# Turning two of three gathered tiles on VectorE instead of TensorE in a mixture-of-experts stage

## The reference, cut to what matters

```
x  = x + tanh(g_xattn) * align(ctx, layernorm(x))
xf = layernorm(x);  logits = xf @ gate_w.T
w, sel = top_k(logits, 2);  w = softmax(w)
out[n] = sum over the 2 chosen e of w[n,e] * (expert_w[e] @ xf[n])
x  = x + tanh(g_ffn) * out
```

## Time and profile before

| | us |
|---|---|
| median of 3 runs (599.56, 602.33, 602.07) | 602.07 |
| the profiled execution, its own time | 599.65 |
| its span | 597.9 |
| TensorE busy | 457.6 (77%) |
| VectorE busy | 307.6 (51%) |
| ScalarE busy | 263.0 (44%) |
| GpSimd busy | 225.5 (38%) |

### The profile page before, as it was taken

The page is one execution under the profiler, slowest core; times in us unless marked ns, Lnnn a source line. Parts: engine busy times, 40 slices in busy tenths (PEclk is TensorE's granted clock), DMA queues, the critical chain, the costliest instruction groups (busy, mean ns, idle before and its releaser), DMA issues. The chain is left out here.

```text
span 597.9 us, 8208 instructions
## 1 busy us (share of the span) xinstructions
PE 457.6 (77%) x2029; PEld 271.4 (45%) x2029; DVE 307.6 (51%) x1635; ACT 263.0 (44%) x508; POOL 225.5 (38%) x214
## 2 busy tenths in 40 slices
PE   8989655477232304687996989999999999999980
PEld 7989543254122201343443544444454444445440
DVE  7778799999998885898678411101111010111000
ACT  6538778854735402892653223322233332223320
POOL 5550222000000000003428565766657665767522
PEclk9999868668565655796997999999999999999995
DMA  8965334640046001777999686878868787878743
GB/s 289 353 189 190 86 85 117 187 98 2 0 160 263 1 1 36 288 245 231 296 260 309 116 164 122 149 134 144 138 114 153 130 142 136 139 122 152 118 53 35
DMA packets 61386, 88.88 MB, mean 149 GB/s; under 512 B 24933, under 2 KB 25189, under 8 KB 61181
## 3 DMA queue, kind: packets, MB, share of 16 engines
q0 software_dynamic: 16048, 37.31, 35.8%
q1 hardware_dynamic: 38701, 42.64, 21.8%
q10 hardware_dynamic: 6592, 8.42, 4.5%
HBM read 48.92 MB, written 39.43 MB: 148 GB/s over the span
## 5 line engine op out<-in xcount | busy, mean ns | idle before, releaser
L1973 PE MATMUL psum<-big,work 128*128 x560 | 257.1, 602 | 4.3 <-ACT work L1627 4.3
L697 POOL DMA_INDIRECT stage<-x_rows,row_ids x71 | 70.0, 986 | 224.1 <-DVE row_ids L1173 176.0
L1973 PEld LDWEIGHTS psum<-big,work 128*128 128x128 f32 x560 | 102.9, 194 | 108.0 <-issue 108.0
L1323 DVE TENSOR_TENSOR part_scale<-stage,st 128x1 f32<-128x1 f32 x62 | 10.0, 162 | 201.2 <-DMA stage<-x_rows,row_ids 201.2
L717 POOL DMA_INDIRECT out_dram<-prow,row_ids x34 | 61.3, 1802 | 36.0 <-ACT prow L1638 14.2
L717 POOL DMA_INDIRECT out_dram<-tokens,row_ids x36 | 57.2, 1589 | 41.3 <-DMA out_dram<-tokens 15.5
L1638 ACT ACTIVATE tokens<-psum,tile_shares 128x512 f32<-128x512 f32 x36 | 24.7, 687 | 98.4 <-issue 70.5
L1638 ACT ACTIVATE prow<-psum,tile_shares 128x512 f32<-128x512 f32 x34 | 23.3, 687 | 86.8 <-issue 78.6
L1947 PEld LDWEIGHTS psum<-ident,stage 128*128 128x128 f32 x284 | 35.6, 143 | 40.6 <-issue 33.7
L1756 PE MATMUL psum<-ident,stage 128*128 128x128 f32 x128 | 27.7, 401 | 33.3 <-ACT big L1526 20.5
L1627 ACT COPY work<-psum 128x512 f32<-128x512 f32 x71 | 41.0, 578 | 19.2 <-PE psum L1947 14.8
(11 more groups left out here) (388 smaller groups left out, 649.7 us busy)
## 6 DMA issues: line engine op xcount, KB each, us to landing
tokens<-in_x_dram SPq DMA_DIRECT2D x16, 1024.0 KB, 11.8
stage<-in_L_ffn_expert_w_dram ACTq DMA_DIRECT2D x8, 1024.0 KB, 5.6
out_dram<-tokens SPq DMA_DIRECT2D x8, 1024.0 KB, 9.1
x_rows<-tokens SPq DMA_DIRECT2D x7, 1024.0 KB, 7.3
tokens<-dist_rows SPq DMA_DIRECT2D x52, 64.0 KB, 2.1
dist_rows<-work SPq DMA_DIRECT2D x16, 160.0 KB, 2.0
dist_rows<-prow SPq DMA_DIRECT2D x5, 256.0 KB, 10.5
stage<-x_rows,row_ids POOLq DMA_INDIRECT x71
```

Of the source, the lines that this page charges most:

```text
L697: pool.indirect_dma_start(out=xin[:, n % UX, :], out_offset=None, in_=x1_d[0:T, :] if n < FA else x1_d[:, :], in_offset=bass.IndirectOffse ...
L1973: ins = nc.tensor.matmul(psum[:, UP + n % UP, :], xinT[:, n % UX, c, :], expT[:, bass.ds(own, 1), c, :].rearrange("p o d -> p (o d)"), sta ...
```

## The change

Of the second list, tiles 12 and 13, 15 and 16, and so on to 69 and 70 (20 pairs, `PAIRED` holds the first of each) aren't turned by TensorE. VectorE turns a pair with 16 transposes: a block of 32 partitions of the gathered tiles, in blocks of 32x32 numbers, goes to 32 partitions of `pairT`, so that the four chunks of 128 columns of both tiles are done in one instruction (32 partitions x 256 numbers). `pairT` is three pairs in `x[:, 4:10, :]`, and the expert matmuls read it directly. Tiles 0 to 11 and 14, 17, ..., 68 (31, `TURNED`) go as before. The second list gathers into six buffers (UZ = 6) in an order in which the two of a pair lie side by side, with semaphores of their own, six tiles ahead instead of four.

```diff
+    UZ = 6
+    UD = 6
+    HOMES = (4, 5, 3, 1, 2, 0)
+    PAIRED = [n for n in range(FA + 3, NSEQ - 1) if (n - FA) % 3 == 0]
+    TURNED = [n for n in range(NSEQ) if n not in PAIRED and n - 1 not in PAIRED]
...
-        xin = stagef[:, 0:UX * RW].rearrange("p (h c) -> p h c", c=RW)
+        xin = stagef[:, 0:UZ * RW].rearrange("p (h c) -> p h c", c=RW)
+        pairT = x[:, GT:GT + UD, :]
...
+        def home(n):
+            return n % UX if n < FA else HOMES[(n - FA) % UZ]
+
+        def landed(n):
+            return (s_xi[n % UX], 16 * (n // UX + 1)) if n < FA else (s_zi[(n - FA) % UZ], 16 * ((n - FA) // UZ + 1))
+
+        def pair_of(n):
+            return PAIRED.index(n if n in PAIRED else n - 1)
+
+        def tileT(n, c):
+            if n in TURNED:
+                return xinT[:, n % UX, c, :]
+            return pairT[:, (2 * pair_of(n) + (n not in PAIRED)) % UD, c * P:(c + 1) * P]
...
-                if n >= UX:
+                if UX <= n < FA:
                     pool.wait_ge(s_yt, n - UX + 1)
-                if n - UX >= FA:
-                    pool.wait_ge(s_scale, n - UX - FA + 2)
+                if FA <= n < FA + UZ and home(n) < UX:
+                    pool.wait_ge(s_yt, max(m for m in range(FA) if home(m) == home(n)) + 1)
+                if n - UZ >= FA:
+                    if n - UZ in TURNED:
+                        pool.wait_ge(s_yt, TURNED.index(n - UZ) + 1)
+                    else:
+                        pool.wait_ge(s_dt, pair_of(n - UZ) + 1)
+                    pool.wait_ge(s_scale, n - UZ - FA + 2)
...
+            AHEAD = [n + UX for n in range(FA - UX + 1)] + [FA + 2, FA + 3, FA + 5]
+            AHEAD += [min(n + UZ, NSEQ) for n in range(FA, NSEQ + 1)]
...
-                if n + UX < NSEQ:
-                    gather(n + UX)
+                for m in range(*AHEAD[n:n + 2]):
+                    gather(m)
...
+            def turn_pair(n):
+
+                d = 2 * pair_of(n)
+                v.wait_ge(*landed(n))
+                v.wait_ge(*landed(n + 1))
+                if d >= UD:
+                    v.wait_ge(s_y, PAIRED[(d - UD) // 2] + 2)
+                for a in range(P // NB):
+                    for g in range(P // NB):
+                        got = xin[NB * g:NB * (g + 1), home(n):home(n) + 2, 0:C].rearrange("p t (q a i) -> p t q a i", q=CH, i=NB)
+                        to = pairT[NB * a:NB * (a + 1), d % UD:d % UD + 2, :].rearrange("p t (q n) -> p t q n", q=CH)
+                        ins = v.transpose(to[:, :, :, NB * g:NB * (g + 1)], got[:, :, :, a, :])
+                ins.then_inc(s_dt, 1)
...
             for n in range(FA, NSEQ):
+                if n in PAIRED:
+                    turn_pair(n)
                 tile_share(n)
...
             def copy_in(n):
+                if n not in TURNED:
+                    return
+                i = TURNED.index(n)
...
             def turn(n):
-                pe.wait_ge(s_xi[n % UX], 16 * (n // UX + 1))
-                if n >= UP:
-                    pe.wait_ge(s_yc, n - UP + 1)
+                if n not in TURNED:
+                    return
+                i = TURNED.index(n)
+                pe.wait_ge(*landed(n))
+                if i >= UP:
+                    pe.wait_ge(s_yc, i - UP + 1)
...
+            def tile_ready(n):
+                if n in TURNED:
+                    pe.wait_ge(s_yc, TURNED.index(n) + 1)
+                else:
+                    pe.wait_ge(s_dt, pair_of(n) + 1)
```

More of the change, by code:

```diff
@@ L397, in flamingo_block @@
         s_xi = [sem(f"tile_gathered{h}") for h in range(UX)]
+        s_zi = [sem(f"second_tile_gathered{h}") for h in range(UZ)]
+        s_dt = sem("pair_turned")
         s_yt = sem("tile_transposed")
@@ L692, in gather @@
                         pool.wait_ge(s_sto[b], 16)
-                if n >= UX:
+                if UX <= n < FA:
                     pool.wait_ge(s_yt, n - UX + 1)
-                if n - UX >= FA:
-                    pool.wait_ge(s_scale, n - UX - FA + 2)
+                if FA <= n < FA + UZ and home(n) < UX:
[6 more added lines that the diff above has]
+                    pool.wait_ge(s_scale, n - UZ - FA + 2)
                 pool.indirect_dma_start(
-                    out=xin[:, n % UX, :], out_offset=None, in_=x1_d[0:T, :] if n < FA else x1_d[:, :],
+                    out=xin[:, home(n), :], out_offset=None, in_=x1_d[0:T, :] if n < FA else x1_d[:, :],
                     in_offset=bass.IndirectOffsetOnAxis(ap=rows_ids[:, n:n + 1], axis=0),
-                ).then_inc(s_xi[n % UX], 16)
+                ).then_inc(landed(n)[0], 16)
             def add(n):
@@ L1316, in ids @@
                                                  [psum[:, 7, 0:1].ap[0], [2 * JB, K], [1, JB]])))
+            def turn_pair(n):
[10 more added lines that the diff above has]
+                ins.then_inc(s_dt, 1)
             def tile_share(n):
                 j = n - FA
-                v.wait_ge(s_xi[n % UX], 16 * (n // UX + 1))
+                v.wait_ge(*landed(n))
                 v.wait_ge(s_scale, n - FA + 1)
-                lnk(v.tensor_tensor(part_scale[:, :], xin[:, n % UX, C + 1:C + 2], kinds[:, 1, j:j + 1], ALU.mult))
-                v.scalar_tensor_tensor(scale[:, n:n + 1], xin[:, n % UX, C:C + 1], kinds[:, 0, j:j + 1], part_scale[:, :],
+                lnk(v.tensor_tensor(part_scale[:, :], xin[:, home(n), C + 1:C + 2], kinds[:, 1, j:j + 1], ALU.mult))
+                v.scalar_tensor_tensor(scale[:, n:n + 1], xin[:, home(n), C:C + 1], kinds[:, 0, j:j + 1], part_scale[:, :],
                                        ALU.mult, ALU.add).then_inc(s_scale, 1)
@@ L1623, in copy_in @@
             def copy_in(n):
+                if n not in TURNED:
+                    return
+                i = TURNED.index(n)
                 if n >= UX:
                     act.wait_ge(s_y, n - UX + 1)
-                act.wait_ge(s_yt, n + 1)
-                nc.scalar.copy(xinT[:, n % UX, :, :].rearrange("p c n -> p (c n)"), psum[:, n % UP, :]).then_inc(s_yc, 1)
+                act.wait_ge(s_yt, i + 1)
+                nc.scalar.copy(xinT[:, n % UX, :, :].rearrange("p c n -> p (c n)"), psum[:, i % UP, :]).then_inc(s_yc, 1)
             def copy_out(n):
@@ L1942, in turn @@
             def turn(n):
-                pe.wait_ge(s_xi[n % UX], 16 * (n // UX + 1))
-                if n >= UP:
-                    pe.wait_ge(s_yc, n - UP + 1)
+                if n not in TURNED:
[4 more added lines that the diff above has]
+                    pe.wait_ge(s_yc, i - UP + 1)
                 for c in range(CH):
-                    ins = nc.tensor.transpose(psum[:, n % UP, c * P:(c + 1) * P], xin[:, n % UX, c * P:(c + 1) * P],
+                    ins = nc.tensor.transpose(psum[:, i % UP, c * P:(c + 1) * P], xin[:, home(n), c * P:(c + 1) * P],
                                               ident[:, :])
                 ins.then_inc(s_yt, 1)
+            def tile_ready(n):
[3 more added lines that the diff above has]
+                    pe.wait_ge(s_dt, pair_of(n) + 1)
             def owned(n):
@@ L1956, in last_expert @@
             def last_expert(n, own):
-                pe.wait_ge(s_yc, n + 1)
+                tile_ready(n)
                 pe.wait_ge(s_ye, n - UP + 1)
@@ L1960, in last_expert @@
                     for c in range(CH):
-                        ins = nc.tensor.matmul(psum[:, UP + n % UP if h == 0 else 4, h * HC:(h + 1) * HC], xinT[:, n % UX, c, :],
+                        ins = nc.tensor.matmul(psum[:, UP + n % UP if h == 0 else 4, h * HC:(h + 1) * HC], tileT(n, c),
                                                expT[:, bass.ds(own, 1), c, h * HC:(h + 1) * HC].rearrange("p o d -> p (o d)"),
@@ L1972, in expert @@
                 for c in range(CH):
-                    ins = nc.tensor.matmul(psum[:, UP + n % UP, :], xinT[:, n % UX, c, :],
+                    ins = nc.tensor.matmul(psum[:, UP + n % UP, :], tileT(n, c),
                                            expT[:, bass.ds(own, 1), c, :].rearrange("p o d -> p (o d)"),
```

## The result

The changed kernel takes 582.12 us (median of 4 runs, 581.6 to 583.19), the kernel before 600.98 us in the same comparison: ratio 0.9689, 95% interval 0.9657 to 0.972. The forecast was 583.5 us. The profiled execution has a span of 579.8 us, 18.1 less than before.

What follows compares the result with a forecast made beforehand. TensorE was taken to bound the second list's stage. 18.2 us from turns removed, less 0.7, is 17.5 us: 582.2 from the profiled execution, 584.6 from the median, so 583.5 us forecast, range 580 to 596 us.

Steps and rivals of the forecast that it cites:

- The price of a turn: TensorE, second list: each turn costs 0.43 us by tile distance; 36 tiles after the first two give 15.5 us.
- The first pair: Tiles 12 and 13: without turns and the wait for gather 12, tile 12 can start 2.74 us earlier.
- 0.7 us for a late landing: First pair: half of the 1.5 us wait that the late bound for gather 13's landing would give, taken off.
- The sum: Whole kernel: 18.2 us gained up to tile 67, less 0.7, is 17.5 us.
- The cover I gave (74%): VectorE in steady state: 8.0 us of work per three tiles, 74% of TensorE's 10.75 us.
- cover of 8.8 us: GpSimd, add 9 to add 67: alone it could reach add 67 at 543.3, TensorE releases it at 552.1.
- 7 x 2.70: GpSimd: seven flagged adds each wait 2.70 us more for the add ahead to land.
- The end: Last adds: a chain of flagged adds waiting for landings; what TensorE gains after tile 67 is worth nothing.
- A: GpSimd becomes the bound through slower landings and longer flagged-add waits: smaller gain, 589 or 597 us; chance 0.17.
- B: VectorE becomes the bound: 0.69 us a transpose, 12.3 us per three tiles, about 612 us; chance 0.10.
- C: VectorE's transposes hold GpSimd: 0.13 us an instruction, 589 us, or some 80 us lost if held throughout; chance 0.07.
- D: No change: possible only by a long stall at the first pair with the clock halved, 5 to 8 us; chance 0.04.

Runs made afterwards that it cites:

- dead turns: Changed kernel, with four unread TensorE transposes of the identity for each paired tile in place of the turns removed: 599.56 us, ratio 0.9984.
- seven of nine: Changed kernel with 7 of 9 tiles turned by VectorE, still six gather buffers and gathers six tiles ahead: 583.27 us, ratio 0.9706.
- two kernels with 24 transposes: Changed kernel with eight extra unread transposes a pair: each right before its twin, 592.43 us; all eight behind the sixteen, 611.89 us.
- with sums: Changed kernel with four unread VectorE sums of two SBUF inputs among each pair's last transposes: 584.27 us, ratio 0.9737.
- four of five: Changed kernel with four of five tiles turned by VectorE, five gather buffers in turn, gathers five tiles ahead: 588.36 us, ratio 0.9804.

## Why the prediction was right

*The price of a turn.* The mechanism forecast is the one seen: TensorE is full, and what it no longer has to do comes off the time (dead turns bring it back). From tile 12's matmuls to tile 68's it was 216.86 us before (352.63 in the earlier trace rows, 569.49 in the earlier trace rows) and is 200.61 now (350.93 to 551.54). 37 turns are gone in between: 16.25 us, 0.44 each, for 0.43 in the prediction. Taking it from the distance of tiles, and not from the 273 ns of each transpose, is what made the sum.

*The first pair.* Timeline of GpSimd where the second list begins, before and after:

```profile
331.24 1.01 POOL L697 DMA_INDIRECT stage<-x_rows,row_ids  x1 [2.34 <-DVE half_row_ids L1313]
```

```profile
332.43 1.02 POOL L725 DMA_INDIRECT stage<-x_rows,row_ids  x1 [2.32 <-DVE half_row_ids L1343]
```

Counted from this first gather, tile 12 starts 2.9 us earlier, for 2.74 predicted. I had taken off 0.7 us for a late landing; it was not needed, but with 0.6 us to spare it was near.

*The sum.* From the first gather to add 67 it was 239.02 us before (331.24 to 570.26) and is 220.32 now (332.43 to 552.75): 18.7 us, for 18.2 in the sum before the 0.7 was taken off. The medians differ by 18.9. So the step that was off is the 0.7, and the 1.4 us between forecast and result is less than single executions of the kernel before differ by (599.56 to 602.33 us). The base had some luck in it: the forecast lay midway between two times of the kernel before, 599.65 and 602.07, and the median of the comparison, 600.98, lies there too.

*VectorE.* 436 ns for a transpose and 0.449 from one to the next, 7.2 us a pair, for 0.42 and 6.7. The length was right to 4% by the row of the same size; the step from one to the next is 13 ns more, which was left out. 31.97 of 40 us for "about 30". The cover I gave (74%) is 80%: (7.18 + 1.4) of 10.75 us.

*GpSimd.* Same durations, and it did wait for ScalarE before add 67. But the cover of 8.8 us was a term that I had too large. Seven waits for a landing cost 22.4 us beyond the gaps of 0.30, not 7 x 2.70 = 18.9: six of the flagged adds come 5.9 to 6.4 us after the one ahead, and the seventh (544.59) waits 4.88 us, since no gather stands between it and the add ahead any more. Another 1.7 us went to the shares that queue behind the first pair's turn (the gather at 351.55), where I had put nothing. What is left at the end is the wait for ScalarE, 2.0 us beyond the gap. That was enough here, and it is gone with seven of nine.

*The end.* Turns of tiles 69 and 70 give nothing: add 67 to 68 is 5.65 us in the changed kernel, longer than any tile.

*The rivals.* A did not decide in this kernel, and does in the next step up. B did not decide either, since 0.449 us an operation is under the 0.59 from which I had the gain shrink. The two kernels with 24 transposes bear out its limits: 11.19 us per three tiles, as much as 16 operations of 0.61 us would make, shrank the gain (592 us), and 12.15, or 0.67 us an operation, gave 612 us, what I had put beside 12.3. C is out for transposes. The Trainium skill ("SBUF — State Buffer", Reading the diagram) has the shared pair of ports taken by VectorE operations in a two-port mode and by those with two SBUF inputs, the latter only against a GpSimd operation that reads SBUF. That GpSimd's instructions were 9 to 17 ns longer with sums, and not longer with transposes, agrees in sign; no run shows what the indirect DMAs read, or a lock as such. D is out: the first pair held nothing up.

Three expectations failed. With 24 transposes the step was that extra operations cost as much as those in place; they overlapped with their twins. With four of five and with seven of nine it was that more turns taken from TensorE would still come off the time. With seven of nine the rival was right, not faster than the changed kernel, and the adds at the end took the gain; with four of five neither reading had a loss, and half of it is TensorE waiting for VectorE.

## What to carry to other kernels

Price work on a full engine by the distance of two repeats, one with it and one without, in the same trace; durations of pipelined matmuls overstate it (273 ns each where 110 are paid). An engine that is slower at a task is still the right place for it while its whole round fits under the round of the full engine; work out that share, and how much of the next engine's cover is left, since the first step takes most of it. When a gain stops, look at what released the last instruction of the neighbour: here add 67's wait for ScalarE vanished in the same step in which the gain did.

## What the runs showed of the hardware

Two transposes that follow each other on VectorE without a wait, with the same input block and the same output block of 32 partitions, take 0.775 us; where the input block is another one it is 0.449 each, 0.898. By this alone 24 operations per pair took 9.8 or 10.8 us, and the kernel 592 or 612 us. The Trainium skill has it as a model ("VectorE: DVE Perf Modes", Two Vector instructions with no wait between them): an operation whose start quadrant differs from the last one's, on either side, starts only when all earlier ones have finished. The trace agrees where the input block differs; no run has two that differ in the output block alone. The twins of these runs also read the same numbers, which could be the reason by itself. Against that, a share and the transpose behind it, which read other numbers but both start at partition 0, overlap too (changed kernel, VectorE):

```profile
351.62 0.22 DVE L1368 SCALAR_TENSOR_TENSOR tile_shares<-stage,st,part_scale 128x1 f32<-128x1 f32 x1
351.75 7.17 DVE L1359 STREAM_TRANSPOSE tokens<-stage 32x256 f32<-32x256 f32 x16
```

Each of the 16 transposes of the changed kernel differs from its neighbour in the input block, so each pays the full step. By the rule of that page no order of the 16 avoids it, since no two have both blocks in common; another order was not run.

A transpose of 32x256 float32 numbers took 436 ns, and a sum of the same size 416.
